# Attention bias in PSUM: ScalarE copies three heads, TensorE adds one

## What is computed

```python
scores = jnp.einsum('bhid,bhjd->bhij', q, k) * scale
diag = i - j
in_band = (diag >= 0) & (diag < 256)
bias = jnp.where(in_band, learnable_bias[:, jnp.clip(diag, 0, 255)], 0.0)
scores = jnp.where(diag >= 0, scores + bias[None], -jnp.inf)
m = jnp.maximum(jnp.max(scores, axis=-1), off)
p = jnp.exp(scores - m[..., None])
denom = jnp.sum(p, axis=-1) + jnp.exp(off - m)
out = jnp.einsum('bhij,bhjd->bhid', p, v) / denom[..., None]
```

## Time and profile before

| | us |
|---|---|
| median of 3 runs (1793.2 to 1794.51) | 1794.21 |
| the profiled execution | 1794.08 |
| its span, first to last instruction | 1792.3 |
| TensorE busy (9136 matmuls) | 1639.8 |
| VectorE busy | 1291.7 |
| ScalarE busy (1596 instructions) | 1109.9 |
| GpSimd busy | 249.4 |
| mean granted TensorE clock | 0.957 |

### The profile page before, as it was taken

The page is one execution under the profiler, slowest core; times in us unless marked ns, Lnnn a source line. Parts: engine busy times, 40 slices in busy tenths (PEclk is TensorE's granted clock), DMA queues, the critical chain, the costliest instruction groups (busy, mean ns, idle before and its releaser), DMA issues. The chain is left out here.

```text
span 1792.3 us, 28802 instructions
## 1 busy us (share of the span) xinstructions
PE 1639.8 (91%) x9136; PEld 762.4 (43%) x9136; DVE 1291.7 (72%) x3801; ACT 1109.9 (62%) x1596; POOL 249.4 (14%) x123
## 2 busy tenths in 40 slices
PE   7999999669999999999999999999999998777763
PEld 3444444213444444444444444444444443333321
DVE  2444544398887888888888788878888833589996
ACT  2333333205878778778887887877878886344432
POOL 4323323210000000000000000000000000244443
PEclk9999999858999999999999999999999999899995
DMA  5444444842453444335335334433533202122211
GB/s 210 141 156 155 140 160 151 193 95 48 84 85 60 84 72 73 80 64 84 80 58 90 81 53 78 93 58 66 105 57 57 53 15 76 35 77 76 70 47 47
DMA packets 124628, 157.09 MB, mean 88 GB/s; under 512 B 14928, under 2 KB 80528, under 8 KB 124240
## 3 DMA queue, kind: packets, MB, share of 16 engines
q1 hardware_dynamic: 124496, 155.45, 37.2%
HBM read 104.15 MB, written 50.46 MB: 86 GB/s over the span
## 5 line engine op out<-in xcount | busy, mean ns | idle before, releaser
L876 ACT ACTIVATE probs<-ps 128x1024 f32<-128x1024 f32 (+3 forms) x768 | 592.2, 810 | 176.7 <-PE ps L685 118.3
L1166 DVE CUSTOM_DVE_ANT_0 junk<-ps,bias_q 128x384 bf16<-128x384 f32 (+2 forms) x1024 | 501.6, 502 | 138.1 <-PE ps L660 127.6
L660 PE MATMUL ps<-k_stack,q_stack 96*128 96x384 bf16 (+3 forms) x1536 | 501.4, 344 | 30.8 <-DVE mx L1166 16.3
L679 PE MATMUL ps<-q_stack,k_stack 99*128 99x512 bf16 (+3 forms) x1536 | 489.6, 328 | 13.2 <-ACT ps L891 4.7
L1159 DVE TENSOR_REDUCE mx<-ps 128x1 f32<-128x128 f32 (+3 forms) x768 | 364.6, 485 | 42.4 <-PE ps L660 35.1
L685 PE MATMUL ps<-bias_r,ident_r 128*128 128x384 f32 (+2 forms) x1280 | 352.6, 363 | 0.0
L636 PE MATMUL ps<-attn 128*128 128x512 f32 x768 | 332.2, 595 | 10.9 <-DMA attn<-hT 9.9
L700 PE MATMUL ps<-probs,v_sb 128*32 128x512 f32 (+3 forms) x3072 | 327.3, 498 | 0.1
L660 PEld LDWEIGHTS ps<-k_stack,q_stack 96*128 96x128 bf16 x1536 | 143.0, 97 | 379.8 <-DVE mx L1166 149.8
L685 PEld LDWEIGHTS ps<-bias_r,ident_r 128*128 128x128 f32 x1280 | 222.4, 193 | 37.1 <-issue 0.3
L636 PEld LDWEIGHTS ps<-attn 128*128 128x128 f32 x768 | 146.5, 191 | 195.8 <-issue 195.8
(11 more groups left out here) (90 smaller groups left out, 1068.6 us busy)
## 6 DMA issues: line engine op xcount, KB each, us to landing
q_stack<-q_parts SPq DMA_DIRECT2D x192, 128.0 KB, 4.3
v_dram<-v_sb SPq DMA_DIRECT2D x32, 512.0 KB, 2.7
v_sb<-v_dram SPq DMA_DIRECT2D x32, 512.0 KB, 9.6
q_parts<-q_stack SPq DMA_DIRECT2D x96, 128.0 KB, 1.9
k_parts<-k_stack SPq DMA_DIRECT2D x96, 128.0 KB, 2.0
k_stack<-k_parts SPq DMA_DIRECT2D x32, 384.0 KB, 7.3
attn<-hT SPq DMA_DIRECT2D x8, 1024.0 KB, 6.3
k_stack<-k_parts SPq DMA_DIRECT2D x32, 256.0 KB, 8.0
```

The source lines that it names most:

```text
L660: pe.matmul(ps_ring[:, use.bank, 0:c1 - c0], q_stack[0:STACK, b, hl, I * P:(I + 1) * P], k_stack[0:STACK, b, hl, c0:c1], start=True, stop= ...
L679: mm = pe.matmul(ps_s[:, u % 2, hh, 0:w], k_stack[0:ROWS, b, hl, J * P:(J + 1) * P], q_stack[0:ROWS, b, hl, i0:i0 + w], start=not in_bank, ...
L876: act.activation(probs[:, (u // 2) % 3, 2 * pr:2 * pr + 2, 0:w], ps_s[:, pr, :, 0:w], ACT.Exp).then_inc(exp_done, 1)
L1166: ins = dve.tensor_tensor_reduce(out=junk[:, use.bank, 0:c1 - lo], in0=ps_ring[:, use.bank, lo - c0:c1 - c0], in1=bias_q[:, hl, BAND - t0 ...
```

## The change

ScalarE now writes the bias of heads 1, 2 and 3, and TensorE adds only head 0's. bias_s holds three heads, bias_r one. `seed` takes a unit instead of a tile: for an odd unit it writes both banks as before, for an even one only head 1's bank. `seed_after` now runs after every exp, and seeds the unit two ahead. `scores` waits for `seeded` in every banded unit, before head 0's score too. GpSimd's three operations per group get one head, one head and three heads instead of two each.

```diff
-        bias_s = sb("bias_s", [P, 2, 2, BAND])
-        bias_r = sb("bias_r", [P, 2, 2, 2, BAND], FP32R)
+        bias_s = sb("bias_s", [P, 2, 3, BAND])
+        bias_r = sb("bias_r", [P, 2, 2, 1, BAND], FP32R)
...
-                in_bank = bw and u % 2
-                if in_bank:
-                    pe.wait_ge(seeded, n * NBAND + BANDED.index(u // 2) + 1)
+                if bw:
+                    pe.wait_ge(seeded, 2 * (n * NBAND + BANDED.index(u // 2)) + u % 2 + 1)
                 for hh in range(2):
                     hl = 2 * (u % 2) + hh
+                    in_bank = bw and hl
...
-            def seed(g, T, done=0):
-                c, J, i0, w = tile_cols(T)
-                b0, bw = band_cols(T)
-                if T == 0:
+            def seed(g, u, done=0):
+                c, J, i0, w = tile_cols(u // 2)
+                b0, bw = band_cols(u // 2)
+                pr = u % 2
+                heads = slice(1 - pr, 2)
+                nh = 1 + pr
+                if u < 2:
                     act.wait_ge(bias_split, 3 * (g + 1))
                 act.wait_ge(exp_done, FIRST + done)
                 act.sem_inc(act_passed, 1)
                 if w > bw:
-                    act.activation(ps_s[:, 1, :, bw:w], zero[:, :].unsqueeze(2).broadcast_to([P, 2, w - bw]),
-                                   ACT.Copy)
-                act.activation(ps_s[:, 1:2, :, 0:bw], bias_s[:, bass.ds(g % 2, 1), :, b0:b0 + bw], ACT.Copy)\
+                    act.activation(ps_s[:, pr, heads, bw:w],
+                                   zero[:, 0:nh].unsqueeze(2).broadcast_to([P, nh, w - bw]), ACT.Copy)
+                act.activation(ps_s[:, pr:pr + 1, heads, 0:bw],
+                               bias_s[:, bass.ds(g % 2, 1), pr:1 + 2 * pr, b0:b0 + bw], ACT.Copy)\
                     .then_inc(seeded, 1)
             def seed_after(g, n, u, more):
-                if u % 2 and u + 2 < NU:
+                if u + 2 < NU:
                     if u // 2 + 1 in BANDED:
-                        seed(g, u // 2 + 1, n * NU + u + 1)
-                elif u % 2 and more:
-                    seed(*more, 0, n * NU + u + 1)
+                        seed(g, u + 2, n * NU + u + 1)
+                elif more:
+                    seed(*more, u % 2, n * NU + u + 1)
...
             seed(0, 0)
+            seed(0, 1)
```

More of the change, by code:

```diff
@@ L1049, in take_bias @@
                 lo = bias_r[:, slot, 1, :, :].rearrange("p a h c -> p (a h) c")
-                pool.tensor_copy(hi, bias_in[:, 0:2, ::-1]).then_inc(bias_split, 1)
+                pool.tensor_copy(hi, bias_in[:, 0:1, ::-1]).then_inc(bias_split, 1)
                 pool.wait_ge(bias_split, 3 * g + 1)
-                pool.tensor_tensor(lo, bias_in[:, 0:2, ::-1], hi.bitcast(FP32), ALU.subtract)\
+                pool.tensor_tensor(lo, bias_in[:, 0:1, ::-1], hi.bitcast(FP32), ALU.subtract)\
                     .then_inc(bias_split, 1)
-                pool.tensor_copy(bias_s[:, slot, :, :].rearrange("p a h c -> p (a h) c"), bias_in[:, 2:HG, ::-1])\
+                pool.tensor_copy(bias_s[:, slot, :, :].rearrange("p a h c -> p (a h) c"), bias_in[:, 1:HG, ::-1])\
                     .then_inc(bias_split, 1)
```

## The result

The changed kernel takes 1887.92 us (1886.22 to 1889.47, 4 runs) against 1794.36: the ratio is 1.0523, 95% interval [1.0504, 1.0541]. Its profiled execution has a span of 1887.2 us, 94.9 more than before.

The account below looks back on a forecast made before the run. Bound tile by tile by ScalarE or TensorE, coupled through two PSUM slots, with VectorE limiting T2, T3. 30 batches at +2.75 (82 us), the last two 9.6, start 0.5: 1794 + 92 = 1886, said as 1885; range 1850 to 1912.

Parts of the forecast that it names:

- Stretches: One attention batch cut at its tiles: T4 2.30, T5-T8 15.4, T9-T10 5.15, T11-T0 6.8, T1 2.7, T2-T3 4.95 us.
- forecast trim of 0.2: Batch sum: 37.3 us cut to 37.1, because some 0.2 came from terms rounded upwards.
- T9, T10: Two attention tiles: 5.15 us taken, bounds 4.65 and 5.27, TensorE coming in late after waiting for seeds.
- T2, T3: Two attention tiles: 4.95 us taken, bounds 4.7 and 5.15, part of TensorE's relief becoming a wait for VectorE.
- Relief by 2.70, load by 6.7 us: Per batch: TensorE loses 2.70 us of bias matmuls; ScalarE gains 6.7 us of seeds, fills and gaps.
- The last two batches: Batches without maxima, 29.91 us before: ScalarE decides nearly everywhere, 34.7 us, +4.8 each, 9.6 together.
- third rival: TensorE's clock falls in attention because of idle holes: 1935 us and above, chance 0.09.
- Start and sum: First score waits for fill and seed, +0.5 us once; with 82 for 30 batches and 9.6, sum +92 us.
- The slack averages out: Rival over all attention: only engine totals count, a batch of some 32.5 us, time 1743 us; chance 0.08.
- Half-elastic: Rival: TensorE works ahead enough in ScalarE's tiles to halve its later stretches, 1794 to 1815 us; chance 0.05.
- The clock falls: Third rival: a third of attention at 1.2 GHz lengthens T9, T10, T2, T3; 1935 us and above; chance 0.09.

Follow-up runs that it names:

- one-copy run: One copy from a zero-padded bias table replaces fill and copy: in the changed kernel (T0, T7, T8) 1871.42 us; in the kernel before (T0, T8) 1794.16 us.
- added-alone run: The changed kernel with TensorE still adding head 1's bias, which ScalarE writes as well: 1901.52 us, ratio 1.0598.
- the run with both of its operations light: The kernel before without head 1's bias matmuls, and VectorE's row maxima cut to 64 columns in both operations: 1716.01 us, ratio 0.9563.
- the relief alone: The kernel before with head 1's bias matmuls left out and nothing in their place: 1757.5 us, ratio 0.9793.

## Why the prediction was right

It gave 1885 us and a range of 1850 to 1912; measured were 1887.92. The mechanism, that ScalarE's own time decides in the full tiles and the relief of TensorE is worth little elsewhere, was right; that the total came within 3 us is partly luck. Step by step:

- *Stretches.* Forecast 2.30, 15.4, 5.15, 6.8, 2.7, 4.95, trimmed to 37.1; measured 2.31, 15.23, 5.16, 6.66, 2.69, 5.04, together 37.09. Those in which ScalarE decides are right by its own instruction costs, two of them a little high (0.17 and 0.14), mostly because an exp with a seed behind it takes 1.12, not 1.14. The forecast trim of 0.2 covered that. The prediction also read ScalarE as already at its limit in T11 and T0 of the kernel before; the one-copy run there shows a tie with TensorE in T11. With the added seeds on ScalarE this made no difference.
- *T9, T10.* I took 5.15 with TensorE deciding, as measured. The relief was put at up to 0.6 there, of which TensorE's late start was guessed to eat most. The added-alone run measured it: 0.36 us in T9 and T10, while the load alone had lengthened the two by 0.25 (5.27 to 5.52).
- *T2, T3.* Taken 4.95, measured 5.04. The reason named, VectorE and its ring, held in the kernel before, where the run with both of its operations light showed it. I had given the relief 0.2 us; the stretch fell by 0.11, of which the added-alone run gives the relief 0.03 (5.08 without it).
- *Relief by 2.70, load by 6.7 us.* Measured as they act: the load alone adds 3.18 us a batch (34.35 to 37.53), the relief alone saves 1.17, and on top of the load 0.44. Net 2.74, forecast 2.75.
- *The last two batches.* This term was mis-sized in its parts. The round without maxima took 36.82 us where 34.7 stood; the fall of the clock accounts for 1.89 of that, and without it 34.93 would be left. The prediction had a falling clock only in its third rival. The piece behind that round is not a whole round, which I overlooked; it grew by 3.2 (from 1487.61 to 1508.56 before, 24.2 us from 1579.49 after). Together +10.1 (6.9 + 3.2) where 9.6 stood: the two errors cancelled, by luck.
- *Start and sum.* The first exp comes 1.07 us later, of which 0.74 lies ahead of the first seed, in work that the change doesn't touch; 0.33 remain of the 0.5. The last phase takes 283.5 us, before 283.7. 1.1 + 83.9 (30 rounds from the first T4 to the last but one) + 10.1 make 95.1 of the 94.9 us. Where 83.9 was measured the prediction had 82: the thirtieth round, half of it without maxima, grew by 4.1 (32.06 to 36.13) and not by 2.75.
- *Rivals.* "The slack averages out" would have needed 1743: the gaps are real (1.12 us in each row), and the one-copy run shows that ScalarE's time in full stretches is paid nearly one for one. "Half-elastic" (1794 to 1815) is out too: what T9, T10 and T2, T3 gave back is 0.22 us a batch. "The clock falls" had a real mechanism, but in the steady batches the granted clock stayed at 1.00, although TensorE waits up to 1.01 us at a time; in the last two rounds it fell and cost some 2.4 us (0.55 + 0.76 + 1.13). The rule of the Trainium skill to work first on the engine with the highest occupancy ("Perfetto Trace Analysis", section "Identifying the Most-Contended Engine"), taken as plainly as the prediction took it, would have approved. The same section wants TensorE judged by its weight loads rather than its matmuls, and these were 43% of the span. Here even the relief for nothing brought 37 us of the 86 that were taken off TensorE. For the 128-column copy the Trainium skill's page "ScalarE: Activation LUTs" (section "What ACT_TABLE_LOAD costs") led to an estimate of 0.20 us; the trace has 0.20.

## What to carry to other kernels

When two engines hand work to each other through two buffers, cut one round into its tiles and sum the larger of the two engines' times tile by tile; totals, shares and averages miss both the full tiles and the idle ones. Work moved to an engine that is at its limit in some tiles is paid there in full, and its relief elsewhere is partly met by the next limit (here a ring of three banks that VectorE empties). In an ordered queue a new item also delays those behind it, so slack in an engine is not yet room for work.

## What was not expected of the hardware

The clock of TensorE fell to 0.58 granted for stretches of 4 and 7 us in a round where it was still busy 28.47 of 36.82 us and never waited more than 1.4 us for ScalarE; in steady rounds with 32.29 of 37.09 busy it stayed at 1.00. T6 of that round had 0.64 granted and took 4.69 us; T6 of the next round, with the same instructions, had 1.00 and took 3.93. A ScalarE copy of 1024 columns from SBUF to PSUM held the engine 0.97 us, an exp of 1024 columns from PSUM to SBUF with another behind it 0.92.
